# A state-space scan and an expert layer on one core: small work moved behind its inputs, the projection and step size spread over three steps

## What is computed

```
# part 1: state-space layer on ctx, gated by layernorm(x)
xin   = in_proj @ ctx                        # 256 channels
u     = silu(causal_conv4(xin) + conv_b)
dt, Bm, Cm = split(x_proj @ u, 8, 16, 16)
delta = softplus(dt_proj @ dt + dt_proj_b)
A     = -exp(A_log)                          # 256 x 16
state = state * exp(delta * A) + delta * u * Bm      # over 256 rows, 16 states
y     = (sum over states of state * Cm + D * u) * silu(layernorm(x))
x1    = x + y
# part 2: expert layer, 8 experts, the best 2 for each row
xn    = layernorm(x1)
gate, expert = top2(softmax(xn @ Wg))
pos   = running count of rows in the expert; kept if pos < 320
out   = x1 + sum over both of gate * (relu(xn @ w1[expert]) @ w2[expert])
```

## Time and profile before

| | us |
|---|---|
| three executions, median | 313.26 |
| lowest, highest | 311.56, 313.32 |
| the profiled execution | 314.71 |
| its span in the trace | 312.6 |

### The profile page before, as it was taken

One profiled execution on the slowest core, in us unless ns is written; L12 is line 12 of the kernel. 1 busy time (PEld: TensorE's weight loads), 2 busy tenths in 40 slices (PEclk: granted clock), 3 DMA queues, 4 the chain that ended last, 5 costly groups with the idle time before them and its releaser, 6 DMA issues. The chain is left out here.

```text
span 312.6 us, 4937 instructions
## 1 busy us (share of the span) xinstructions
PE 264.2 (85%) x1520; PEld 232.9 (75%) x1520; DVE 218.2 (70%) x383; ACT 170.0 (54%) x367; POOL 218.7 (70%) x182
## 2 busy tenths in 40 slices
PE   8969877886957947697699899999999999999960
PEld 7748665755746636576488799999999999999950
DVE  2489999987699788998945346857575757566610
ACT  1678579463893457638404347646473737373410
POOL 1839699959939699698371686677777777777652
PEclk9995989596796976756559999999999999999995
DMA  6459540052001442110055144454555454644011
GB/s 171 172 142 338 167 170 0 3 191 113 0 17 54 163 155 122 51 53 0 34 199 181 64 103 163 176 210 167 209 167 208 166 207 165 208 166 167 33 40 38
DMA packets 14929, 40.24 MB, mean 129 GB/s; under 512 B 2906, under 2 KB 9756, under 8 KB 11968
## 3 DMA queue, kind: packets, MB, share of 16 engines
q1 hardware_dynamic: 11648, 33.02, 31.2%
q0 software_dynamic: 2816, 6.32, 5.8%
q10 hardware_dynamic: 448, 0.70, 0.9%
HBM read 32.58 MB, written 8.49 MB: 131 GB/s over the span
## 5 line engine op out<-in xcount | busy, mean ns | idle before, releaser
L342 POOL TENSOR_TENSOR dbu<-du,bsb 128x1024 f32<-128x1024 f32 x31 | 72.5, 2359 | 6.2 <-ACT bsb L515 3.6
L1131 DVE TENSOR_TENSOR_SCAN h<-ps,dbu 128x512 f32<-128x512 f32 x64 | 74.5, 1206 | 1.1 <-ACT ps L529 0.7
L529 ACT ACTIVATE ps<-delta,anegs 128x255 f32<-128x255 f32 x128 | 53.0, 462 | 7.5 <-DVE h L1131 7.3
L1296 DVE SCALAR_TENSOR_TENSOR htlo<-ps,hthi 128x320 fp32r<-128x320 f32 x64 | 30.5, 487 | 35.2 <-ACT hthi L655 35.2
L766 PE MATMUL ps<-cst,hc 128*128 128x128 f32 x256 | 48.4, 351 | 0.0
L749 PE MATMUL ps<-stack,sels 64*128 64x256 f32 x64 | 19.5, 393 | 33.1 <-DVE hc L1142 29.6
L426 POOL TENSOR_TENSOR w2lo<-w2raw,w2hi 128x512 fp32r<-128x512 f32 x30 | 38.4, 1303 | 9.8 <-ACT w2hi L646 9.6
L766 PEld LDWEIGHTS ps<-cst,hc 128*128 128x128 f32 x256 | 39.4, 182 | 4.6 <-issue 2.2
L749 PEld LDWEIGHTS ps<-stack,sels 64*128 64x128 f32 x64 | 12.3, 239 | 40.6 <-issue 40.5
L935 PE MATMUL ps<-hthi,w2hi 128*128 128x320 f32 x128 | 40.3, 315 | 0.0
L935 PE MATMUL ps<-xthi,w1hi 128*128 (+1 forms) x128 | 40.2, 314 | 0.0
(11 more groups left out here) (149 smaller groups left out, 482.1 us busy)
## 6 DMA issues: line engine op xcount, KB each, us to landing
w1raw<-in_w SPq DMA_DIRECT2D x8, 1024.0 KB
w2raw<-in_w SPq DMA_DIRECT2D x8, 1024.0 KB, 4.8
bsb<-b_rows SPq DMA_DIRECT2D x7, 1024.0 KB, 7.3
expert_rows<-fill SPq DMA_DIRECT2D x1, 2580.0 KB, 15.9
xe<-expert_rows SPq DMA_DIRECT2D x8, 258.0 KB, 5.3
out<-x SPq DMA_DIRECT2D x4, 256.0 KB, 4.9
xnat<-in_x SPq DMA_DIRECT2D x1, 768.0 KB, 7.4
xe<-expert_rows SPq DMA_DIRECT2D x8, 64.5 KB, 5.5
```

Of the source, the lines that this page charges most:

```text
L342: nc.gpsimd.tensor_tensor(dbu[j % DRING][:], du[:, :, None, cols(b)].to_broadcast([P, EC, 2, L]), bsb[b % 2][:, None, 2 * p:2 * p + 2, :]. ...
L529: ins = nc.scalar.activation(decays(g % SLOTS_DA)[:, c, i * L + 1:(i + 1) * L], delta[:, c, b * L + 1:(b + 1) * L], ACT.Exp, scale=anegs[: ...
L1131: nc.vector.tensor_tensor_scan(h[g % HRING][:, c].rearrange("p n t -> p (n t)"), decays(g % SLOTS_DA)[:, c, :], dbu[g % DRING][:, c].rearr ...
L1296: nc.vector.scalar_tensor_tensor(out=htlo[:, f, :], in0=ps[:, f % 4, 0:CAP], scalar=0.0, in1=hthi[:, f, :].bitcast(F32), op0=ALU.max, op1= ...
```

## The change

Six things change. The bias of batch 0's step size leaves TensorE: it comes as one more column of the channel constants, ScalarE adds it in Abs, VectorE in a new operation; keep-busy matmuls stand in the place of the bias matmuls. From batch 1 on, the projection is done two batches ahead, at step 7, and the step size is cut into bias and first part (step 0) and second part (step 1), with ScalarE's part of the softplus at step 2; so the work for one batch is spread over three of TensorE's steps. GpSimd's parts of the softplus, and z's rstd, come a turn later. The turned x1 is formed a step earlier and the choice a step later; placing is cut in two (`place`, `weigh`). The scatters are sent by single tiles: batch 0's two tiles ahead of dbu 21 and 25, batch 1's ahead of dbu 30 and 31, batch 2's after the last dbu and after w1's low parts. In batch 3, z is turned at step 1, w1's high parts are formed in two pairs at steps 1 and 4, x is turned into the bank at step 5, and at the end four keep-busy matmuls go and a wait for the slots moves behind the selection matmuls.

```diff
@@ constants
-NCH = ALOG + DS
+DTB = ALOG + DS
+NCH = DTB + 1
-V0BANK = DABANK + 3
+V0BANK = DABANK + 2
@@ GpSimd
-            def send(b):
+            def send(j):
+                b = j // BT
                 pool.wait_ge(s["gates_done"], b + 1)
                 pool.wait_ge(s["slots_done"], b + 1)
...
             for j in range(1, STEPS):
                 b, p = divmod(j - DRING, PAIRS)
+                if b >= 1 and p == 0:
+                    add_x(b - 1)
+                if b >= 1 and p == (1 if b == B - 1 else 2):
+                    row_rstd(b - 1)
                 if b >= 0 and b + 1 < B:
-                    if p == (2 if b else 3):
+                    if p == 3:
                         softplus_d(b + 1)
                         softplus_w(b + 1)
-                    if p == 3:
+                    if p == 4:
                         softplus_delta(b + 1)
                         delta_u(b + 1)
-                if b == 0 and p == 4:
+                if b == 0 and p == 5:
                     z_rstd(2, slice(BT, TILES))
-                if b >= 1:
-                    if p == 0:
-                        add_x(b - 1)
-                    if p == (1 if b == B - 1 else 2):
-                        row_rstd(b - 1)
-                    if p == 7:
-                        if b == 1:
-                            pool.wait_ge(s["xe_filled"], 16)
-                        send(b - 1)
+                if b == 2 and p in (1, 5):
+                    if p == 1:
+                        pool.wait_ge(s["xe_filled"], 16)
+                    send(0 if p == 1 else 1)
+                if b == 3 and p in (2, 3):
+                    send(p)
                 drive(j)
-            send(B - 2)
             for m in range(WP):
...
+            for j in tiles_range(B - 2):
+                send(j)
             row_rstd(B - 1)
             pool.wait_ge(s["xe_in"], 32)
-            send(B - 1)
+            for j in tiles_range(B - 1):
+                send(j)
@@ ScalarE
-                nc.scalar.activation(spe, by_chunk(bank), ACT.Abs).then_inc(s["sp_abs"], 1)
-                act.wait_ge(s["sp_abs"], b + 1)
+                    nc.scalar.activation(spe, by_chunk(bank), ACT.Abs).then_inc(s["sp_abs"], 1)
+                else:
+                    for c in range(EC):
+                        nc.scalar.activation(spe[:, c, :], ps[:, bank + c, 0:L], ACT.Abs,
+                                             bias=ch[:, c, DTB:DTB + 1]).then_inc(s["sp_abs"], 1)
+                act.wait_ge(s["sp_abs"], EC + b)
...
                     if p == (1 if b else 2):
                         b_rows(nb)
                         hi_rows(nb)
+                    if p == 2:
                         decay_exps(nb, WBANK)
                         logs(nb)
                 if b >= 1:
-                    if p == (2 if b == B - 1 else 4):
+                    if p == (2 if b == B - 1 else 3):
                         x1_turned(b - 1)
                     if p == (3 if b == B - 1 else 5):
                         row_scales(b - 1)
-                        top_exp(b - 1)
                         for j in range((b - 1) * BT, b * BT):
                             normalise(j)
-                if b == B - 1 and p == 5:
-                    for m in range(WP):
-                        split_w1(0, m)
-                if p == (7 if b < B - 2 else 6):
+                    if p == (4 if b == B - 1 else 6):
+                        top_exp(b - 1)
+                if b == B - 1 and p in (1, 4):
+                    for m in range(WP // 2):
+                        split_w1(0, m + (WP // 2 if p == 4 else 0))
+                if p == (7, 7, 6, 2)[b]:
                     z_turned(b)
@@ TensorE
+            def first_dt(k):
+                for c in range(EC):
+                    ins = nc.tensor.matmul(ps[:, V0BANK + c, 0:L], wdt[:, k, c * P:(c + 1) * P], u[:, k, cols(0)],
+                                           start=(k == 0), stop=(k == EC - 1))
+                return ins
+            keep_clock(2, BBANK)
             pe.wait_ge(s["dts_in"], 16)
...
-            dt_bias(V0BANK)
+            keep_clock(6, BBANK)
...
-                ins = dt_part(0, k, V0BANK)
+                ins = first_dt(k)
...
                 if b >= 1:
-                    if p == (2 if b == B - 1 else 4):
+                    if p == (3 if b == B - 1 else 4):
                         logits(b - 1)
-                    if p == (3 if b == B - 1 else 5):
+                    if p == (4 if b == B - 1 else 6):
                         counts(b - 1)
                 if g + 1 < STEPS:
                     c_cast(g + 1)
-                else:
-                    pe.wait_ge(s["slots_done"], B - 1)
-                    turn(xnat[:, tiles_of(B - 1), :], True, False)
...
-                if nb < B and p == (0 if b else 1):
-
-                    pe.wait_ge(s["u_done"], EC * (nb + 1))
...
+                if b >= 1 and nb < B:
+                    if p == 0:
                         pe.wait_ge(s["zt_done"], b)
-                    if b >= 2:
-                        pe.wait_ge(s["slots_done"], b - 1)
-                    project(nb, XBANK[nb])
-                    dt_bias(WBANK)
-                    dt_part(nb, 0, WBANK)
-                    dt_part(nb, 1, WBANK).then_inc(s["v_psum"], 1)
+                        dt_bias(WBANK)
+                        dt_part(nb, 0, WBANK)
+                    if p == 1:
+                        dt_part(nb, 1, WBANK).then_inc(s["v_psum"], 1)
...
-                if p == (6 if b + 2 < B else 5):
+                if p == (6, 6, 5, 1)[b]:
...
+                if b == B - 1 and p == 5:
+                    pe.wait_ge(s["slots_done"], B - 1)
+                    turn(xnat[:, tiles_of(B - 1), :], True, False)
+                if b + 2 < B and p == 7:
+                    if b:
+                        pe.wait_ge(s["slots_done"], b)
+                    project(b + 2, XBANK[b + 2])
-                if b >= 1 and p == (1 if b == B - 1 else 3):
+                if b >= 1 and p == (1 if b == B - 1 else 2):
...
             place_rows(0)
-            keep_clock(4, DABANK)
             counts(B - 1)
             place_rows(1)
-            pe.wait_ge(s["slots_done"], B)
-            pe.wait_ge(s["zt_done"], B)
...
+            pe.wait_ge(s["slots_done"], B)
             expert(0, True, False)
@@ VectorE
+            for c in range(EC):
+                dve.wait_ge(s["sp_abs"], c + 1)
+                nc.vector.tensor_scalar(spt[:, c, :], ps[:, V0BANK + c, 0:L], ch[:, c, DTB:DTB + 1], 0.0,
+                                        ALU.add, ALU.max).then_inc(s["sp_relu"], 1)
...
-            softplus_t(0, V0BANK)
+            dve.wait_ge(s["sp_relu"], EC)
+            nc.vector.tensor_tensor(spt, spt, spe, ALU.add).then_inc(s["sp_t"], 1)
...
-                    if p == (2 if b else 3):
-                        softplus_t(nb, WBANK)
...
                     if p == (1 if b == B - 1 else 2):
                         variance(b - 1, row_stats(b - 1))
-                    if p == (2 if b == B - 1 else 4):
+                if nb < B and p == (2 if b else 3):
+                    softplus_t(nb, WBANK)
+                if b >= 1:
+                    if p == (3 if b == B - 1 else 5):
                         choose(b - 1)
                     if p == (4 if b == B - 1 else 6):
                         place(b - 1)
+                    if p == (5 if b == B - 1 else 7):
+                        weigh(b - 1)
```

More of the change, by code:

```diff
@@ L83, in cols, with tiles_range @@
     return slice(b * L, (b + 1) * L)
+def tiles_range(b):
+    return range(b * BT, (b + 1) * BT)
 def tiles_of(b):
@@ L202, in build @@
             "xp_psum hi_done brow_done brow_out b_lo_in b_hi_in stack_done v_psum "
-            "sp_abs sp_exp sp_ln sp_d sp_t sp_w delta_done du_done a_exp a_neg "
+            "sp_abs sp_relu sp_exp sp_ln sp_d sp_t sp_w delta_done du_done a_exp a_neg "
             "z_stats z_var z_rstd z_mean z_scale zs_done zt_psum zt_done wg_psum wg_done "
@@ L378, in row_rstd @@
                                         ).then_inc(s["ln_rstd"], 1)
-            def send(b):
+            def send(j):
+                b = j // BT
                 pool.wait_ge(s["gates_done"], b + 1)
                 pool.wait_ge(s["slots_done"], b + 1)
[L384 to L390, removed]
+                pool.wait_ge(s["xn_done"], j + 1)
+                for k in range(TOPK):
+                    nc.gpsimd.indirect_dma_start(
+                        xe_dram, bass.IndirectOffsetOnAxis(ap=sloti[:, j, k:k + 1], axis=0),
+                        xrow[:, j, k, :], None, bounds_check=SLOTS - 1, oob_is_err=False
+                    ).then_inc(s["scattered1" if b == B - 1 else "scattered0"], 16)
@@ L585, in _ @@
             nc.scalar.activation(anegs[:], ch[:, :, ALOG:ALOG + DS], ACT.Exp).then_inc(s["a_exp"], 1)
+            act.wait_ge(s["sel_in"], 16)
+            nc.scalar.activation(sels[:], brow[0:XPC, 0:BC], ACT.Copy).then_inc(s["sel_done"], 1)
```

(37 more changed lines are left out.)

## The result

The changed kernel takes 318.58 us (median of 4 runs, 315.49 to 319.13) where the kernel before takes 312.54 beside it: ratio 1.0175, 95% interval 1.0099 to 1.025. It is slower by 1.75%, and the interval does not reach 1; faster, 306.7 us, was forecast. The profiled execution took 318.97 us, its span is 317.2 (before 312.6).

What follows compares the result with a forecast made beforehand. VectorE, the busiest engine in the scan, was taken as the bound, GpSimd close behind. Terms +0.8 +1.6 -4.4 -4.8 +0.2 = -6.6 gave 308.1 us for the profiled execution and 306.7 for the median; range 302.0 to 312.5.

Steps and rivals of the forecast that it cites:

- before the scan: Start to first scan: added keep-busy matmuls and split Abs outweigh the removed bias matmuls, +0.8 us.
- batch 0: Batch 0: z's later rstd delays ScalarE's z silus and scan 9's decay by 1.9 us, +1.6 us in sum.
- Batches 1 and 2: Middle batches: waits for stack rows and logits go, smaller step-size and multiply waits come, -4.4 and -4.8 us.
- Batch 3 to the first expert: Batch 2's gate to first expert: VectorE's savings are given back to late expert rows behind GpSimd's line, +0.2 us.
- At nothing: Items across the kernel costed at zero, such as selector copy, w1's high parts and load order; lost cover 0.2 to 0.7 each.
- The slower one: Rival 2, first expert: TensorE stays at 1.2 GHz after waiting for expert rows, 318.1 us, chance 0.13.
- 7.2 less 2.7: Batch 1: removed waits of 5.1 and 2.1 us less new waits of 1.3 and 1.4, given as -4.4.
- G+41.3 and G+35.3: First expert's start, counted from batch 2's gate G: before, and with the end's savings alone.
- Rival 4: Before the scan: the added early matmuls lift TensorE's clock before the step size, 305.1 us, chance 0.13.
- Rival 1: Batches 1 and 2: split step size at half clock, VectorE waits 2.4 and 3.0 us longer, 312.1 us, chance 0.17.
- The end: Batch 3 to first expert: late scatters, rows in at G+34.2, TensorE idle 3.4 to 4.8 us, start at G+41.5.

Runs made afterwards that it cites:

- e1_psum: Changed kernel with slots and place term passed through PSUM and ScalarE forming the gates of batches 0 to 2: 306.42 us, ratio 0.9754.
- e4_prologue_only: Kernel before with only the new start of batch 0 (bias by ScalarE and VectorE, keep-busy matmuls for bias matmuls): 312.7 us, ratio 0.994.
- e5_psum_w1_behind: e1_psum with GpSimd's four w1 low parts moved behind batch 2's four scatters: 304.9 us, ratio 0.9728.
- e3_sends_only: Kernel before with only GpSimd's new order of scatters and w1 low parts: 324.53 us, ratio 1.0346.
- e7_sends_psum: e3_sends_only with e1_psum's edit (slots and places in PSUM, gates of batches 0 to 2 by ScalarE): 318.94 us, ratio 1.0195.
- e2_w1_behind: Changed kernel with GpSimd's four w1 low parts behind batch 2's scatters again: 315.23 us, ratio 1.0044.
- e11_keep: e1_psum with z's rstd a turn earlier, plus nine keep-busy matmuls ahead of TensorE's wait for the expert rows: 301.28 us, ratio 0.9524.

## Why the prediction was wrong

By stages, in us of the profiled executions against the earlier trace rows; e1_psum is the change without the stall:

| stage | predicted | changed kernel | e1_psum |
|---|---|---|---|
| before the scan | +0.8 | -2.0 | -2.0 |
| batch 0 | +1.6 | +3.0 | +3.0 |
| batch 1 | -4.4 | -0.3 | -3.9 |
| batch 2 | -4.8 | -0.5 | -4.9 |
| batch 3 to first hidden matmul | +0.2 | +3.9 | -0.9 |
| experts | 0 | +0.5 | +0.6 |
| sum | -6.6 | +4.6 | -8.1 |

**The step that failed** stands under "Batches 1 and 2" and "Batch 3 to the first expert": GpSimd's new order was costed as a line of its own (28.5 us, scatters late), and VectorE's choosing, placing and weighing as instructions of their old length, "in its line". Their length rested on GpSimd standing still beside them, which the waits of GpSimd for VectorE's gates showed in the trace of before. Moving those waits away was taken as free. It cost VectorE 12.9 us: 1.83 in batch 1, 4.28 in batch 2, 6.78 in batch 3. With them gone, e1_psum's span is 12.7 us shorter, though not every microsecond is theirs: in batch 1 TensorE's clock also differs (the wait at the softplus term is 2.68 us, 1.41 in e1_psum), and in batch 3 part of the stall only covered a wait for the rows (0.50 us, 1.81 in e1_psum). "At nothing" should have had a sentence on the instructions' lengths; none of the rivals had it either. The slower one blamed TensorE's clock in the first expert, and the experts took 0.5 us longer, not 4; that its 318.1 us is so near the 318.58 measured is chance.

That e1_psum, 306.42 us, is so near the forecast of 306.7 is partly chance too: its terms missed by -2.8, +1.4, +0.5, -0.1, -1.1 and +0.6. The prediction's own additions are off by little: 7.2 less 2.7 is 4.5, not 4.4, and what it lists as saved at the end adds up to 5.7 us, for the 6.0 between G+41.3 and G+35.3.

**Before the scan**: mis-sized and of the other sign. Rival 4 was right, the added matmuls lift the clock and the step size takes 1.97 us where the earlier trace rows has 3.78. But I summed this term to the first scan and not to the gate: in the changed kernel's trace the gain is lost again in batch 0, in a wait for the gate weights that I had not listed. e4_prologue_only and e5_psum_w1_behind did not lose it, so this is one outcome of several, and its odds are not known.

**Batch 0**: the mechanism was right. ScalarE waited 2.34 us for z's rstd and scan 9 waited 2.11 (1.9 forecast). The other 1.3 us of the +3.0 are the wait for the gate weights, 1.81 us, 0.49 before.

**Batches 1 and 2**: right once the stall is away. Gate to gate is 35.3 and 32.1 us in e1_psum, 34.7 and 32.2 forecast. In batch 1 the softplus term waits 1.41 (1.3 forecast), multiply 13, at 80.66, waits 0.60 (1.4 forecast) and the one at 66.83 waits 1.26 (not forecast). Rival 1 got as far as batch 1 in the changed kernel: bias and first part of its step size took 2.07 us each at half clock, the second part 1.91, and the wait was 2.7.

**The end**: right in mechanism. In e1_psum the last scatter ends 28.1 us after gate 2 (28.5 forecast), the rows are in at 32.7 (34.2), the first hidden matmul starts at 40.4 (41.5). TensorE's wait for the rows was too long in the forecast, 3.4 to 4.8 us, and is 1.81; from the rows to the first hidden matmul it then takes 7.7 us (7.0 forecast at half clock). In the changed kernel the gates that release the scatters came at 27.4 us after gate 2 instead of the 20.6 forecast, the stalled multiply ahead of them, the rows were in at 37.7, and the first hidden matmul started at 45.1.

## What to carry to other kernels

An engine that stands waiting may be what keeps its neighbour fast. Before moving work of GpSimd, list which VectorE instructions will run beside it, and of those the ones with two inputs in SBUF and the copies and casts between SBUF tiles; put one operand in PSUM, or let ScalarE do it. Sum an edit to the next place where the engines meet, not to the first instruction that starts earlier. And before a trace is held against another, compare a stretch in which the two kernels are the same: here it differed by 1.9 us (e1_psum and e5_psum_w1_behind) and by 2.2 (e3_sends_only and e7_sends_psum).

## What the runs showed of the hardware

A VectorE multiply of two SBUF tiles, or a cast from SBUF to SBUF, of 0.17 to 0.19 us took 1.15 to 6.97 us beside GpSimd. Instructions with one SBUF input that are neither copy nor cast (a reduction of 0.16 us, a reciprocal of 0.17) were not held. A plain copy between SBUF tiles was, L1322 in e2_w1_behind, at 184.12: 1.11 us for 0.17 in the kernel before, to the end of GpSimd's run at 185.21. Mostly the hold lasted to the end of GpSimd's run of instructions, not of the one that it met: the multiply of 6.97 us passed four boundaries between instructions, the gate multiply of 4.45 us one. In batch 1 the multiply got in at a boundary twice, in the changed kernel at 88.1 us, where the third dbu of the run from 81.11 ends, and in e2_w1_behind at 87.7, where the third of its run from 80.66 does; there the cast right behind it was held to the end of the run:

```profile
88.02 0.19 DVE L1242 TENSOR_TENSOR ohc<-oh,place_of 128x32 f32<-128x32 bf16 x1
```

```profile
86.17 1.55 DVE L1242 TENSOR_TENSOR ohc<-oh,place_of 128x32 f32<-128x32 bf16 x1
87.76 0.19 DVE L1244 TENSOR_REDUCE slot<-ohc 128x4 f32<-128x32 f32 x1
87.98 2.02 DVE L1245 CAST sloti<-slot 128x4 uint32<-128x4 f32 x1
```

What decides that, no run here shows. Where the run ended with dbu 31, in e2_w1_behind, GpSimd then waited and VectorE was free after 2.09 us.

The second thing is the granted clock of TensorE, of which two points stay open: after the same idle of 3.09 us it fell in some executions and stayed up in others, and it fell ahead of the selection, in e11_keep after 18 keep-busy records and only 0.29 us idle.
